# The last stage's stores split between two issuing queues: ConvNeXt block and quantised depthwise convolution

## The reference, cut to what matters

```python
# layer 0: ConvNeXt block
y = depthwise_conv7x7(x) + dw_b                  # per channel
y = layer_norm_over_channels(y) * ln_w + ln_b    # per pixel
y = gelu(y @ w1 + b1)                            # 96 -> 384
gx = sqrt(sum(y*y over pixels)); nx = gx / (mean(gx) + eps)
y = gamma * (y * nx) + beta + y
z = x + (y @ w2 + b2)                            # 384 -> 96
# layer 1: quantised depthwise convolution
w  = sign(w) * 2 ** round(log2(clip(|w|)))       # powers of two
zq = clip(floor(z * 65536) / 65536)
out = depthwise_conv3x3(zq, w) + quantised_bias
```

## Time and profile before

| | |
|---|---|
| median of 3 runs | 1053.07 us (1052.21 to 1053.91) |
| profiled execution | 1059.81 us |
| its span | 1057.9 us |
| PE busy | 978.0 us (92%) |
| VectorE busy | 812.8 us (77%) |
| ACT busy | 764.3 us (72%) |
| POOL busy | 415.8 us (39%) |
| DMA, mean over the span | 178 GB/s |

### The profile page before, as it was taken

One profiled execution on the slowest core, in us unless ns is written; L12 is line 12 of the kernel. 1 busy time (PEld: TensorE's weight loads), 2 busy tenths in 40 slices (PEclk: granted clock), 3 DMA queues, 4 the chain that ended last, 5 costly groups with the idle time before them and its releaser, 6 DMA issues.

```text
span 1057.9 us, 22787 instructions
## 1 busy us (share of the span) xinstructions
PE 978.0 (92%) x6342; PEld 696.6 (66%) x6342; DVE 812.8 (77%) x1477; ACT 764.3 (72%) x1379; POOL 415.8 (39%) x357
## 2 busy tenths in 40 slices
PE   5899999999999179999999999999999859898987
PEld 4688888888888166666666666666666436666655
DVE  5578888888887488888888888888887757666666
ACT  3588888888887277788898988888888616545553
POOL 2577777777776164333332333333332001111110
PEclk9699999999999677999999999999999979989999
DMA  8566666766662582555555555555542357778786
GB/s 187 139 201 199 200 199 197 203 200 200 199 206 62 147 226 78 175 165 165 160 173 165 170 161 177 162 165 172 160 139 80 90 165 217 237 242 247 242 249 209
DMA packets 110261, 188.47 MB, mean 178 GB/s; under 512 B 17357, under 2 KB 104036, under 8 KB 107268
## 3 DMA queue, kind: packets, MB, share of 16 engines
q1 hardware_dynamic: 106132, 183.18, 59.2%
q10 hardware_dynamic: 4096, 4.90, 1.9%
HBM read 129.77 MB, written 58.25 MB: 178 GB/s over the span
## 4 chain that ended last, share of the span: by engine, by line
PE 73%; SPq 10%; DMA 7%; issue 4%; DVE 3%; ACT 2%; POOL 1%; ACTq 0%; DVEq 0%; POOLq 0%
PE psum L659 26%; PE psum L735 22%; PE psum L725 6%; PE psum L726 6%; PE psum L727 6%; PE psum L677 4%; SPq L364 4%; SPq L422 4%; PE psum L631 3%; DMA arena<-z_scratch 2%; SPq L376 2%; DMA arena<-in_x_dram 2%; DMA z_scratch<-arena 1%; DMA arena_r<-y_scratch 1%; ACT arena L848 1%
## 5 line engine op out<-in xcount | busy, mean ns | idle before, releaser
L659 PE MATMUL psum<-arena_r 112*128 112x464 f32 x1536 | 391.5, 395 | 25.9 <-DMA arena<-z_scratch 13.5
L659 PEld LDWEIGHTS psum<-arena_r 112*128 112x128 f32 x1536 | 279.9, 192 | 78.7 <-issue 29.7
L735 PE MATMUL psum<-arena,w2s 128*96 128x448 f32 x672 | 268.4, 544 | 2.8 <-DVE w2s L1097 2.8
L881 ACT ACTIVATE arena<-psum,b1g 128x448 f32<-128x448 f32 x336 | 202.7, 631 | 61.6 <-PE psum L727 61.6
L563 POOL TENSOR_TENSOR arena_r<-arena,arena_r 96x448 fp32r<-96x448 f32 x112 | 137.0, 1223 | 267.4 <-DVE arena_r L1058 193.7
L735 PEld LDWEIGHTS psum<-arena,w2s 128*96 128x96 f32 x672 | 110.2, 164 | 120.8 <-issue 112.9
L725 PE MATMUL psum<-arena_r,w1h 96*128 96x448 f32 x336 | 153.7, 457 | 15.9 <-POOL arena_r L563 15.9
L795 ACT ACTIVATE arena<-psum,bias_a 64x112 f32<-64x112 f32 (+1 forms) x288 | 107.8, 409 | 65.6 <-PE psum L659 52.9
L783 ACT ACTIVATE arena_r<-psum 112x448 fp32r<-112x448 f32 x192 | 93.6, 542 | 78.7 <-PE psum L631 78.5
L552 POOL TENSOR_TENSOR arena<-arena 128x448 f32<-128x448 f32 x96 | 110.8, 1154 | 99.9 <-DVE arena L1013 99.9
L848 ACT ACTIVATE arena<-arena 128x1792 bf16<-128x1792 f32 (+1 forms) x91 | 136.8, 1503 | 2.7
(11 more groups left out here) (100 smaller groups left out, 1107.9 us busy)
## 6 DMA issues: line engine op xcount, KB each, us to landing
arena<-in_x_dram SPq DMA_DIRECT2D x95, 224.0 KB, 5.0
arena<-lines_a SPq DMA_DIRECT2D x46, 448.0 KB
arena<-z_scratch SPq DMA_DIRECT2D x87, 224.0 KB, 4.0
y_scratch<-arena SPq DMA_DIRECT2D x96, 196.0 KB, 4.8
arena<-in_x_dram SPq DMA_DIRECT2D x112, 168.0 KB, 2.6
z_scratch<-arena SPq DMA_DIRECT2D x112, 168.0 KB, 2.0
out_dram<-arena SPq DMA_DIRECT2D x96, 196.0 KB, 3.6
arena_r<-y_scratch SPq DMA_DIRECT2D x98, 168.0 KB, 2.6
```

Of the source, the lines that this page charges most:

```text
L659: mm = nc.tensor.matmul(p_conv[s % 2][:, 0:NCOL], w[:, p, s, TW * k:TW * k + TW], v[:, p, s, slot0 + k:slot0 + k + JP, :].rearrange("p j i ...
L735: mm = nc.tensor.matmul(p_o[k][0:C, 0:CH], w2s[:, p, m, :], hid[p][:, m, CH * t:CH * t + CH], start=(m == 0), stop=(m == MT - 1))
L881: nc.scalar.activation(hid[p][:, m, CH * t:CH * t + CH], p_h[m][:, 0:CH], ACT.Gelu, bias=b1g[:, m:m + 1]).then_inc(gelu_done, 1)
```

## The change

In stage c the stores of channels 1 and 3 of each batch are issued by ACT; those of channels 0 and 2 stay with SP, and so do all stores of stage a. ACT's store of channel s of batch b - 1 stands at the end of step s of batch b. It waits for the same value of `out` as before and adds to the same semaphore. The last batch's two stores come at the end of ACT's program.

```diff
+        def store_channel(eng, S, dst, b, k, p):
+            eng.wait_ge(S["out"], CB * b + k + 1)
+            eng.dma_start(image_runs(dst, CB * b + k), ost[:, p, k, :]).then_inc(S[f"st{p}"], 16)
...
                 def store(b, k, p):
-                    sp.wait_ge(S["out"], CB * b + k + 1)
-                    sp.dma_start(image_runs(dst, CB * b + k), ost[:, p, k, :]).then_inc(S[f"st{p}"], 16)
+                    if S is stages["a"] or k % 2 == 0:
+                        store_channel(sp, S, dst, b, k, p)
...
                             if rows_too and not (first and p == 0 and s < 2):
                                 out_copy(*two_before(b, s, p))
+                            if not rows_too and s % 2 and not (first and p == 0):
+                                store_channel(act, S, out_v, b - 1, s, 1 - p)
                 bodies(act, body)
                 if rows_too:
                     for s in (2, 3):
                         out_copy(NBATCH - 1, s, 1)
+                else:
+                    for s in (1, 3):
+                        store_channel(act, S, out_v, NBATCH - 1, s, 1)
```

## The result

The changed kernel takes 1030.11 us (median of 4 runs, 1028.78 to 1031.37) against 1053.07 us: a ratio of 0.9782 with a 95% interval of 0.9765 to 0.9799, 23.0 us less. The forecast was 1034.6 us, 18.5 us less, in a range of 1027 to 1048. The profiled execution took 1031.37 us, its span 1029.5.

The account below looks back on a forecast made before the run. SP's DMA issues were taken to bound stage c at 7.98 us per batch. New period 6.57 + 0.3 = 6.87: 18 periods gain 20.0 us, five lose 1.5, so 1053.07 - 18.5 = 1034.6 us, range 1027 to 1048.

Parts of the forecast that it names:

- SP's issues bound the stage: In stage c, SP's ten DMA issues per batch, without a wait between them, set the period of 7.98 us.
- SP's new cycle of 6.3 us, a margin of 0.3: Without two stores, SP's issues for a batch in stage c take 6.2 to 6.3 us, 0.3 below PE's 6.57.
- PE is next, at 6.57: Once SP is relieved, PE sets stage c's pace, at 6.57 us per batch as in batches 0 to 3.
- ACT issues under its own copies; the first store delays the copy of the next pair, the second is hidden: On ACT in stage c: first store starts `xt_copy` 0.3 us later per batch, paid by PE; second store costs 0.
- both stores in full: Upper bound for ACT's added cost in stage c: both stores wholly on the path, 1.67 us per batch.
- The sign that was named first: Sign of a right forecast: VectorE's L1185 marks, once per batch, 6.8 to 7.0 us apart from first batch to last.
- The DMA engines suffice: Stage c needs 284 GB/s at 6.87 us per batch; engines had reached 330, so they suffice, with longer flights.
- The rival with 7.33 us per batch: Rival: DMA engines set stage c's pace at 7.33 us per batch; gain 11.7 us, 1041.4 us; chance 0.20.
- the single issue of 1.68 us: One load's issue in the closer-issued phase at 1026:1034, taken as a sign that its queue was full.
- ACT-bound, the slower rival: Rival: ACT's stores make its copies late and PE waits; period 8.24 us, 1066 us in all; chance 0.09.
- The clock: PE's granted clock in stage c: 1.00 expected once stalls go; staying at 0.96 would lose 4.8 us of the gain.
- The end of the stage, 0 plus or minus 0.5: At the end of stage c, the last channel's store follows its copy as before: 0 plus or minus 0.5 us.

Follow-up runs that it names:

- both stores late: Changed kernel with ACT issuing both its stores behind its last copy of the batch, none between second copy and the next pair's copy: 1028.42 us.
- store 1 in two: Changed kernel with ACT's store of channel 1 cut into two DMAs of eight images each: 1051.51 us.

## Why the prediction was right, point by point

*SP's issues bound the stage.* Right, and shown: half the bytes in the stores change nothing, one issue fewer gives 7.13 us, two fewer reach PE's pace, one more goes back to 7.42.

*SP's new cycle of 6.3 us, a margin of 0.3.* Right as far as it can be seen: SP's waits in the changed kernel are 6.2 us in 18 batches, 0.34 per batch.

*PE is next, at 6.57.* Right in kind. The floor is 6.50, in two kernels. The 6.57 was a mean of 6.51, 6.72 and 6.48. The middle one was no slower batch of PE. In the kernel before, PE starts the matmuls of channel 0 at 877.49, 884.00, 890.49 and 896.99, 6.50 us apart. Those of channel 3, whose copy is the mark, start 6.51 us apart where the marks are 6.72 apart, so it is the mark that comes 0.2 us later. The rows of PE itself would have given the 6.50:

```profile
882.14 1.11 PE L659 MATMUL psum<-arena_r 112*128 112x464 f32 x4
...
888.65 1.11 PE L659 MATMUL psum<-arena_r 112*128 112x464 f32 x4
```

*ACT issues under its own copies; the first store delays the copy of the next pair, the second is hidden.* Right in mechanism and place. The size is off, and it is the mis-sized term of the sum: 0.3 us per batch was taken, 0.11 was measured. Two things made it so. The delay is 0.24 us in the mean of the two kinds of batches and not 0.3, since ACT issues this store in 0.57 us and not 0.62. And 0.13 us of it is free. The prediction had it "paid by PE in full" because it read the stall of 0.42 us before the weight load at 952.10 as one for L985. That was a misreading, although the row names L985:

```profile
950.46 1.16 DVE L985 TENSOR_TENSOR arena_r<-psum,arena_r 112x448 fp32r<-112x448 f32 x2 [0.40 <-ACT arena_r L783]
```

L985 ends at 951.62 and the stall runs from 951.68 to 952.10. At the same place in its order PE waits for the next pair's loads; the second of them was issued by SP at 947.90 and landed at 951.98. So the stall belonged to SP's late loads, and it went with them: the kernel with both stores late has none. That a delay on this chain does reach PE was right all the same, as store 1 in two shows, but only past the slack.

Two numbers beside the sum don't follow from its own terms. Without the two stores SP's cycle is 7.98 - 2 x 0.87 = 6.24 us with the usual gap, which the text rounds up to 6.3. And both stores in full are 2 x 0.82 = 1.64 us, not 1.67, or 2.5 by the dearer issue of 1.05 plus 0.2; the forecast uses neither, and of the rivals only the 1066 us rest on the 1.67.

Together, 6.87 was forecast and 6.61 measured, of which 0.07 is PE's own period and 0.19 the stores. That is 18 x 0.26 = 4.7 us, and 1.2 us more come from the five outer periods (0.3 us lost instead of 1.5). With the forecast gain of 18.5 that makes 24.4, beside the 24.3 of the profiled executions. The medians show 23.0; the 1.3 us between are within what a run of this kernel varies by. Both errors lay on the same side, so the gain was understated by a fifth. The sign that was named first, marks 6.8 to 7.0 us apart, did not come: they are 6.6.

*The DMA engines suffice.* Right, with less to spare than it looked: 294 GB/s at a share of 0.93, stores landing in 4.3 us instead of 3.6, and 301 GB/s at 0.95 in the version with both stores late. The rival with 7.33 us per batch is ruled out. What the single issue of 1.68 us waited for stays open. The prediction took it as the sign of a full queue, and no run tests that; at the share of 0.93 the stores' issues last 0.57 to 0.64 us, as before.

*ACT-bound, the slower rival.* It didn't happen, but it was near. A dearer issue ahead of `xt_copy` is what cutting ACT's store in two switches on, and it costs 0.94 us per batch at once. The point from which it makes the kernel slower than before had been put at an added 1.1 us per batch.

*The clock.* As forecast: 1.00 in 880:1000. In the kernel with SP bound again by one more issue it is 0.95 in 900:1000, with 8.5 us in which PE waits for loads.

*The end of the stage, 0 plus or minus 0.5.* From the last mark to the end of the span it is 5.9 us before and after.

## What to carry to other kernels

A queue whose rows follow each other without a wait can be the bound although the DMA engines are not full, and the check is cheap: halve the bytes and keep the issues. In this kernel issues moved to a compute engine were free only in certain places. They ran under that engine's own instruction, but the next instruction, for which another engine waited, started late by what stuck out; the cheapest place was where the engine idled next, behind the last copy of the batch. Before a stall is taken as proof that a chain has no slack, compare the end of the instruction it names with the end of the stall: here they lay 0.48 us apart, and the stall was another's.

## What the runs showed that was not expected

Cutting a store of 112 rows into two of 56 rows made each issue longer, not shorter: 0.75 us instead of 0.63 on SP, 0.67 instead of 0.57 on ACT. Halving the length of the rows left the issue at about its 0.61 us. Why fewer rows take longer was not tried.

The traces show one more difference. The semaphore of a whole store is raised 16 separate times as it lands; that of a half is raised nine times, once 0.2 to 0.3 us after its issue began and eight times as it lands. So the cut changed how a store is spread as well as the number of issues; that a half runs on fewer of the 16 DMA engines would fit, but is not shown. The two readings above don't rest on it. With SP's store in two the chain is SP's issues, and with ACT's in two it is the issues, the copy, its low part and PE.
